# Three seams of a fused decoder layer: later weight quantisation, spread output products, and the feed-forward's first tile quantised one phase earlier

## The reference

```
x = x + self_attention(layernorm(x))            # 16 heads, window 128, sink, grouped output weights
x = x + cross_attention(layernorm(x), context)  # 16 query heads on 4 key heads, 1024 keys, slopes, then @ Wo
x = x + feed_forward(layernorm(x))              # silu(x @ gate) * (x @ up), Hadamard transform, @ down

# feed_forward: every input row is quantised to 8 bits, every weight matrix to three values
act_quant(x):    scale = 128 / max(|x|);         clip(round(x * scale), -128, 127) / scale
weight_quant(w): scale = 1 / mean(|w|);          clip(round(w * scale), -1, 1) / scale
```

## Time and profile before

| | us |
|---|---|
| median of 3 runs | 1656.32 (1654.77 to 1656.93) |
| the profiled execution's own time | 1656.29 |
| span of the profiled execution, first to last instruction | 1654.4 |
| self-attention, markers of steps 0 and 63 | 82.1 and 596.5 |
| cross-attention, first product and last residual row | 612.2 and 1335.4 |
| feed-forward, start | 1336.9 |
| PE busy over the span | 1566.2 (95%) |

### The profile page before, as it was taken

The page is one execution under the profiler, slowest core; times in us unless marked ns, Lnnn a source line. Parts: engine busy times, 40 slices in busy tenths (PEclk is TensorE's granted clock), DMA queues, the critical chain, the costliest instruction groups (busy, mean ns, idle before and its releaser), DMA issues. The chain is left out here.

```text
span 1654.4 us, 23944 instructions
## 1 busy us (share of the span) xinstructions
PE 1566.2 (95%) x7520; PEld 1072.2 (65%) x7520; DVE 1222.6 (74%) x2240; ACT 1186.7 (72%) x1962; POOL 1271.4 (77%) x1138
## 2 busy tenths in 40 slices
PE   8899999999999987999999999999999878999996
PEld 4577777787787755666666666666656425666664
DVE  2489978878776756777877788788778556767765
ACT  2354567777544435999999889989999726877875
POOL 0387767787777723899999999999999928888880
PEclk9999999999999998999999999999999989999999
DMA  7224254332300004210311032102203130110000
GB/s 257 92 80 88 90 136 121 111 122 90 102 20 8 32 18 119 92 46 20 112 39 58 25 107 58 33 19 59 58 13 117 43 114 1 34 33 26 33 14 26
DMA packets 57190, 110.24 MB, mean 67 GB/s; under 512 B 9244, under 2 KB 13596, under 8 KB 56682
## 3 DMA queue, kind: packets, MB, share of 16 engines
q1 hardware_dynamic: 55488, 107.64, 21.2%
q10 hardware_dynamic: 1578, 1.07, 0.2%
HBM read 71.26 MB, written 18.88 MB: 54 GB/s over the span
## 5 line engine op out<-in xcount | busy, mean ns | idle before, releaser
L1374 POOL TENSOR_TENSOR x_p_lo<-x_p,x_p_hi 128x1024 fp32r<-128x1024 f32 x256 | 606.4, 2393 | 62.7 <-ACT x_p_hi L1176 38.4
L1308 DVE TENSOR_REDUCE x_maxes<-x_ps_a 128x1 f32<-128x1024 f32 x252 | 306.6, 1217 | 121.7 <-PE x_ps_a L1459 117.9
L1149 ACT ACTIVATE x_p<-x_ps_b,x_any_valid 128x1024 f32<-128x1024 f32 x256 | 285.1, 1114 | 57.3 <-PE x_ps_b L1439 52.5
L1176 ACT ACTIVATE x_p_hi<-x_p 128x1024 fp32r<-128x1024 f32 x256 | 271.4, 1060 | 6.4
L1439 PE MATMUL x_ps_b<-x_Q,x_K 103*128 103x512 f32 x512 | 216.6, 504 | 9.0 <-ACT x_p L1149 7.2
L1493 PE MATMUL x_ps_o<-x_p_hi,x_V 128*96 128x512 f32 x512 | 209.7, 410 | 4.2 <-POOL x_p_lo L1374 4.2
L1494 PE MATMUL x_ps_o<-x_p_lo,x_V 128*96 128x512 f32 x512 | 202.8, 396 | 0.0
L1459 PE MATMUL x_ps_a<-x_K,x_Q 99*128 99x512 f32 x504 | 168.0, 414 | 11.3 <-DVE x_maxes L1308 8.4
L440 ACT ACTIVATE a_aT_hi<-a_ps_a 128x512 fp32r<-128x512 f32 x64 | 38.3, 598 | 169.5 <-PE a_ps_a L723 146.3
L1439 PEld LDWEIGHTS x_ps_b<-x_Q,x_K 103*128 103x128 f32 x512 | 87.4, 190 | 99.6 <-issue 55.3
L1459 PEld LDWEIGHTS x_ps_a<-x_K,x_Q 99*128 99x128 f32 x504 | 88.8, 190 | 54.4 <-DVE x_maxes L1308 31.9
(11 more groups left out here) (263 smaller groups left out, 4007.3 us busy)
## 6 DMA issues: line engine op xcount, KB each, us to landing
shared<-in_L_ffn_w_gate SPq DMA_DIRECT2D x16, 512.0 KB, 4.3
shared<-in_L_ffn_w_up SPq DMA_DIRECT2D x16, 512.0 KB, 4.1
shared<-in_L_ffn_w_down SPq DMA_DIRECT2D x16, 512.0 KB, 4.4
shared<-in_ctx SPq DMA_DIRECT2D x8, 1024.0 KB, 8.0
x_scratch<-rows SPq DMA_DIRECT2D x31, 256.0 KB, 2.0
x_Q<-x_q_hi SPq DMA_DIRECT2D x112, 64.0 KB, 2.0
shared<-in_L_attn_out_w SPq DMA_DIRECT2D x6, 1024.0 KB, 8.2
ffn_quant<-shared SPq DMA_DIRECT2D x24, 256.0 KB, 4.5
```

The lines of the kernel that those rows point to most:

```text
L1149: act.activation(p[:, v % 3, :, :], ps_b[:, :, :], ACT.Exp, scale=any_valid[:, b % 2:b % 2 + 1]).then_inc(exp_ready, 1)
L1176: act.activation(p_hi[:, r], p[:, v % 3], ACT.Copy).then_inc(hi_ready, 1)
L1308: dve.tensor_reduce(out=maxes[:, c % 2, 3 + r:4 + r], in_=scores_bank(n)[:, :, :], axis=mybir.AxisListType.XY, op=ALU.max).then_inc(max_re ...
L1374: pool.tensor_tensor(out=p_lo[:, v % 3], in0=p[:, v % 3], in1=p_hi[:, r].bitcast(F32), op=ALU.subtract).then_inc(lo_ready, 1)
```

## The change

1. **Weight quantisation.** Load, round, clip, clip and store of chunk k move eight steps later (steps k + 22, k + 24, k + 25, k + 26), and the ring `f_quant` has four places in place of two. The first loads of cross-attention move from step 44 to step 52.
2. **End of cross-attention.** The last batch's output products of groups k = 0, 1 and 2 are spread over units (62, 0) to (64, 1). The inversions of group 14 come in units (61, 3) and (62, 0) to (62, 2), and its `normalise` in (62, 3). The last group is normalised and multiplied in four blocks of 128 columns.
3. **First tile of the feed-forward.** Its layer norm, row maximum, rounding and clipping are made in units (62, 3) to (64, 1) of cross-attention, in `hq_first` and `first_max`. The feed-forward's steps start at -1, with the transposes of `hq_first`.

```diff
@@ self-attention
-        f_quant = shared[:, 6144:7168].bitcast(BF16).rearrange("p (s n) -> p s n", s=2)
+        f_quant = shared[:, 6144:8192].bitcast(BF16).rearrange("p (s n) -> p s n", s=4)
@@ SP
-                if 0 <= c - 18 < FFN_CHUNKS:
-                    store_quant(c - 18)
-                if 0 <= c - 14 < FFN_CHUNKS:
-                    load_raw(c - 14)
+                if 0 <= c - 26 < FFN_CHUNKS:
+                    store_quant(c - 26)
+                if 0 <= c - 22 < FFN_CHUNKS:
+                    load_raw(c - 22)
-                if c == 44:
-                    for j in range(2):
-                        sp.wait_ge(f_stored[j], 16 * (FFN_CHUNKS // 2))
+                if c == 52:
+                    for j in range(4):
+                        sp.wait_ge(f_stored[j], 16 * (FFN_CHUNKS // 4))
@@ ACT (the round and the clip, the same shift for both)
-                if 0 <= c - 16 < FFN_CHUNKS:
-                    k = c - 16
+                if 0 <= c - 24 < FFN_CHUNKS:
+                    k = c - 24
-                    if k >= 2:
-                        act.wait_ge(f_stored[k % 2], 16 * (k // 2))
+                    if k >= 4:
+                        act.wait_ge(f_stored[k % 4], 16 * (k // 4))
@@ DVE
-                if 0 <= c - 17 < FFN_CHUNKS:
+                if 0 <= c - 25 < FFN_CHUNKS:
@@ cross-attention, the spread products
+        last_out = {(HEADS - 2, 0): ((0, 0),), (HEADS - 2, 1): ((0, 2),), (HEADS - 2, 2): ((0, 3),), (HEADS - 2, 3): ((1, 0),),
+                    (HEADS - 1, 0): ((0, 1),), (HEADS - 1, 1): ((1, 2),), (HEADS - 1, 2): ((1, 3),), (HEADS - 1, 3): ((1, 1),),
+                    (HEADS, 0): ((2, 0), (2, 1)), (HEADS, 1): ((2, 2), (2, 3))}
@@ ACT, in the order of a unit: exponential, ACT's copy of PV, then this, then p_hi
+                if (c, r) == (HEADS - 1, 2):
+                    act.wait_ge(first_bias_ready, 1)
+                    act.wait_ge(job_made, jobs_until("Q", 3, B - 1))
+                    act.activation(first_row, ffn_x[0], ACT.Identity, scale=ln_rstd[:, 0:1], bias=ln_bias[:, 0:1]).then_inc(first_row_ready, 1)
+                if (c, r) == (HEADS, 0):
+                    act.wait_ge(first_max_ready, 3)
+                    act.activation(first_row, first_row, ACT.Copy, scale=first_max[:, 2:3], bias=MAGIC).then_inc(first_round_ready, 1)
+                if (c, r) == (HEADS, 1):
+                    act.wait_ge(first_round_ready, 1)
+                    act.activation(hq_first[:, :], first_row, ACT.Relu, scale=-1.0, bias=clip_bias[:, :])
@@ DVE
-                if r == 3 and c >= 5:
+                if r == 3 and 5 <= c < HEADS - 2:
                     inverse((c - 5) // HPG, (c - 5) % HPG)
+                if c == HEADS - 2 and r < 3:
+                    inverse(HEADS // HPG - 2, r + 1)
+                if (c, r) == (HEADS - 2, 3):
+                    dve.wait_ge(ffn_x_in[0], 16)
...
+                    dve.bn_stats(out=stats[:, 0, :], in_=ffn_x[0]).then_inc(stats_ready, 1)
+                    dve.wait_ge(stats_ready, TPB * B + 1)
+                    dve.bn_aggr(out=mv[:, 0, :], in_=stats[:, 0, :]).then_inc(first_mv_ready, 1)
+                if (c, r) == (HEADS - 1, 1):
+                    dve.wait_ge(first_rstd_ready, 1)
+                    dve.tensor_scalar(ln_bias[:, 0:1], mv[:, 0, 0:1], ln_rstd[:, 0:1], -1.0, ALU.mult, ALU.mult).then_inc(first_bias_ready, 1)
+                if (c, r) == (HEADS - 1, 3):
+                    dve.wait_ge(first_row_ready, 1)
+                    dve.tensor_reduce(out=first_max[:, 0:1], in_=first_row, axis=AXX, op=ALU.max, apply_absolute_value=True)\
+                        .then_inc(first_max_ready, 1)
...
+                    dve.tensor_scalar(first_max[:, 1:2], first_max[:, 0:1], EPS_Q, 1.0 / QB, ALU.max, ALU.mult).then_inc(first_max_ready, 1)
...
+                    dve.reciprocal(first_max[:, 2:3], first_max[:, 1:2]).then_inc(first_max_ready, 1)
@@ POOL, after the unit's p_lo
-                if r == 3 and c >= 8 and c % HPG == 0:
+                if r == 3 and 8 <= c < HEADS and c % HPG == 0:
                     normalise((c - 8) // HPG)
+                if (c, r) == (HEADS - 2, 3):
+                    normalise(HEADS // HPG - 2)
+                if (c, r) == (HEADS - 1, 0):
+                    pool.wait_ge(first_mv_ready, 1)
+                    pool.tensor_tensor(out=ln_var[:, 0:1], in0=mv[:, 0, 1:2], in1=eps[:, 0:1], op=ALU.add).then_inc(first_var_ready, 1)
+                    pool.wait_ge(first_var_ready, 1)
+                    pool.tensor_tensor(out=ln_rstd[:, 0:1], in0=ln_var[:, 0:1], in1=half_neg[:, 0:1], op=ALU.pow).then_inc(first_rstd_ready, 1)
-            normalise(HEADS // HPG - 1)
+            for k in range(TPB):
+                cols = slice(k * P, (k + 1) * P)
+                pool.wait_ge(inv_ready, 4 * G + k + 1)
+                pool.tensor_tensor(out=aT[:, G % (GX + 1), cols], in0=num[:, G % 2, cols], in1=den[:, G % 2, cols], op=ALU.mult).then_inc(aT_ready, 1)
@@ PE, in a unit after its PV
+                for k, i in last_out.get((c, r), ()):
+                    G = GX * (B - 1) + k
+                    pe.wait_ge(aT_ready, G + 1)
...
+                    pe.matmul(last_banks[i], aT[:, G % (GX + 1), i * P:(i + 1) * P], wo_sb[:, k, :], start=(k == 0), stop=False)
@@ PE, after the loop (in place of all 16 products)
+            for i in range(TPB):
+                pe.wait_ge(aT_ready, G + i + 1)
+                pe.matmul(last_banks[i], aT[:, G % (GX + 1), i * P:(i + 1) * P], wo_sb[:, GX - 1, :], start=False, stop=True).then_inc(job_made, 1)
@@ feed-forward
-        steps = range(-5, NQ + 18)
+        steps = range(-1, NQ + 18)
-                    pe.wait_ge(hq_ready, m + 1)
+                    if m:
+                        pe.wait_ge(hq_ready, m)
-                        last = pe.transpose(ps_q[:, a, :], hq[:, a * P:(a + 1) * P], ident_bf[:, :])
+                        last = pe.transpose(ps_q[:, a, :], (hq if m else hq_first)[:, a * P:(a + 1) * P], ident_bf[:, :])
```

More of the change, by code:

```diff
@@ L247, in phase_self_attention @@
         f_raw_in = [sem(f"f_raw_in{j}") for j in range(2)]
-        f_stored = [sem(f"f_stored{j}") for j in range(2)]
+        f_stored = [sem(f"f_stored{j}") for j in range(4)]
         f_sum_out, f_all_in = sem("f_sum_out"), sem("f_all_in")
@@ L454, in _ @@
                     act.activation(sink_exp[:, c % 2, :], sink_arg[:, c % 2, :], ACT.Exp).then_inc(sink_exp_ready, 1)
-                if 0 <= c - 16 < FFN_CHUNKS:
-                    k = c - 16
+                if 0 <= c - 24 < FFN_CHUNKS:
+                    k = c - 24
                     act.wait_ge(f_round_ready, k + 1)
-                    if k >= 2:
-                        act.wait_ge(f_stored[k % 2], 16 * (k // 2))
-                    act.activation(f_quant[:, k % 2, :], f_raw[:, k % 2, :], ACT.Relu, scale=-1.0, bias=f_clip[:, :])\
+                    if k >= 4:
+                        act.wait_ge(f_stored[k % 4], 16 * (k // 4))
+                    act.activation(f_quant[:, k % 4, :], f_raw[:, k % 2, :], ACT.Relu, scale=-1.0, bias=f_clip[:, :])\
                         .then_inc(f_clip_ready, 1)
@@ L858, in phase_cross_attention @@
         x1t = rows
+        clip_bias = sb("clip_bias", [P, 1])
+        first_row = hT[:, 1, :]
         ps_a = ps("ps_a", (P, 2, 512))
@@ L889, in phase_cross_attention @@
             sem(n) for n in ("o_copied", "den_copied", "num_ready", "inv_ready", "aT_ready"))
+        first_mv_ready, first_var_ready, first_rstd_ready, first_bias_ready, first_row_ready, first_max_ready, first_round_ready = (
+            sem(n) for n in ("first_mv_ready", "first_var_ready", "first_rstd_ready", "first_bias_ready", "first_row_ready",
+                             "first_max_ready", "first_round_ready"))
         UNITS = [(c, r) for c in range(-2, HEADS + 1) for r in range(4)]
@@ L1506, in _ @@
                         before += 1
+                for k, i in last_out.get((c, r), ()):
+                    G = GX * (B - 1) + k
+                    pe.wait_ge(aT_ready, G + 1)
+                    if k == 0:
+                        if i == 0:
+                            pe.wait_ge(job_read, before)
+                        if i == 1:
+                            pe.wait_ge(max_row_ready, HEADS)
+                        if i >= 2:
+                            pe.wait_ge(max_ready, 4 * HEADS)
+                    pe.matmul(last_banks[i], aT[:, G % (GX + 1), i * P:(i + 1) * P], wo_sb[:, k, :], start=(k == 0), stop=False)
                 if norm_of(c, r):
@@ L1516, in _ @@
                     norms += 1
-            banks = (ps_j[:, :], ps_x[:, :], ps_a[:, 0, :], ps_a[:, 1, :])
-            pe.wait_ge(job_read, before)
-            pe.wait_ge(max_row_ready, HEADS)
-            pe.wait_ge(max_ready, 4 * HEADS)
-            for k in range(GX):
-                G = GX * (B - 1) + k
-                pe.wait_ge(aT_ready, G + 1)
-                for i in range(TPB):
```

(11 more changed lines are left out.)

66 lines of the change are left out of this document (39 added, 27 removed).

## The result

The changed kernel takes 1639.38 us, the median of four runs (1637.48 to 1640.03), against 1655.55 for four runs of the kernel before, taken beside it (1653.37 to 1656.93). The ratio is 0.9902, with a 95% interval from 0.9884 to 0.9919: 16.2 us faster. The forecast was 1637.5, from 18.8 us of gain. The profiled execution took 1639.33, and its span is 1637.5.

What follows compares the result with a forecast made beforehand. It took as bounds ACT's store waits in self-attention, POOL and then PE's leftover products ending cross-attention, and the first tile's chain starting the feed-forward. 1656.3 - 10.5 - 5.5 - 2.8 = 1637.5 us, range 1632 to 1645.

Steps and rivals of the forecast that it cites:

- The quantisation: Self-attention, first batch: ACT's clips no longer wait for `f_quant` stores; gain 10.5 us, at most 11.
- the slack of two steps: Self-attention: store of chunk k - 4 issued two steps, 16 us, before it is needed, so ACT's wait goes.
- the separated loads: Self-attention: absolute-sum loads end in step 21, second loads begin in step 22, so they no longer share DMA engines.
- DVE not short of time: Self-attention, first batch: DVE busy for 59 of 73 us, so not what holds the batch up.
- The end of cross-attention: Cross-attention's tail: last residual row at 1330.6 in place of 1336.08, gain 5.5 us.
- PE's last product takes 1.0 with its drain: End of cross-attention: after the last block's multiply PE finishes at 1329.4; DVE's residual rows set the end, 1330.6.
- rival A: Cross-attention's tail: PE's clock falls, giving 1640.5 us, or 1646.8 if to the block's end; 17 in 100.
- The feed-forward's start: First tile made early: products soon after T (start of the feed-forward's loads), ACT waits for the Hadamard matrix; gain 2.8 us.
- Gain 2.8: Feed-forward's start: silu(1) at T + 9.4 against T + 12.2 before; bounds 1.5 and 5.6 us.
- The sum: Whole kernel: 1656.3 less gains of 10.5, 5.5 and 2.8 gives 1637.5 us.
- the third term: Feed-forward's start: the gain of 2.8 us from making the first tile in cross-attention.
- Rival B: Feed-forward's start gains all 5.6 us, by earlier matrix landing or full clock: 1634.7, at best 1632; 14 in 100.

Runs made afterwards that it cites:

- e1: Kernel before plus only the quantisation change (eight steps later and ring of four): 1643.99 us, ratio 0.9934.
- e2: Kernel before plus only the ring of four for `f_quant`, no step moved: 1647.20 us, ratio 0.9951.
- e3: Kernel before plus only the shift of quantisation by eight steps, ring of two kept: 1643.53 us, ratio 0.9935.
- e7: Changed kernel plus twelve unused score products on PE between its last PV and the last four output products: 1639.50 us, ratio 0.9908.
- e5: Changed kernel with the Hadamard matrix loaded in cross-attention, not at the feed-forward's start: 1630.90 us, and 1629.30 once more.
- e4: Changed kernel without the early first tile, which is quantised in the feed-forward as before: 1638.14 us, ratio 0.9904.
- e11: Changed kernel without the early first tile, but with the Hadamard matrix loaded in cross-attention: 1639.47 us, ratio 0.9904.

## Why the prediction was right, and where it wasn't

**The quantisation** was right in mechanism and size: 10.5 foreseen, 10.4 in the markers, 10.9 by e1's ratio; no wait for a store, 129.46 us against "about 129". The sum was not touched by what e2 and e3 add: the prediction gave the slack of two steps as the reason and the separated loads as a bonus, while either half alone would have won most of it. It also called DVE not short of time, from a busy share of 59 in 73 us; with the ring alone PE stands for DVE 2.80 us (e2), so the shift wins something on DVE's side too.

**The end of cross-attention** was right up to the inversions. Counted from the end of unit 251's `p_lo` (1299.53), the last `p_lo` ends at 11.6 (foreseen 11.8), the last PV at 13.2 (13.35), the inversions at 18.1 (18.2), and ACT's idle time is 3.23 (3.4). The step that was mis-sized is the last: "PE's last product takes 1.0 with its drain". The first two pairs took 2.00 and 1.89 each at the lower clock, so the last row came at 22.4 in place of 20.9, and 3.9 were won where 5.5 were foreseen (4.1 when counted from the exponential of unit 254 to T). That is a small form of rival A. The prediction looked for the clock's fall where only PV is left; it came behind the hole of 3.10 us that the spreading itself makes, while POOL and DVE work on the last group. e7 filled that hole, and the same products ran at 1.00. The rule that it quoted against A was "activity releases the throttle" (the Trainium skill, "TensorE: Matmul & The Clock Gate", Part 1). The traces of after and e7 agree with it, read from its other side: a rest was followed by 0.50, work by 1.00. But in e5 the same hole of 3.11 us was followed by 1.00, so the rule alone does not say what one hole will cost.

**The feed-forward's start** was right in its steps: landing 8.5 us after issue (8.7 foreseen), products at T + 1.2 (1.3), ACT idle for 5.41 (about 5), silu(1) at T + 9.05 (9.4). The Trainium skill ("DMA: Bandwidth & Descriptors", "Issuing engines are not separate DMA queues") says that DMAs which the scalar, sync and GpSimd engines issue run on the same 16 DMA engines and interleave. The trace agrees: the matrix on ACT's queue landed (8.5 us) with SP's 2 MB (8.3 us) and not ahead of it. The step that failed is "Gain 2.8", and for two reasons. First its base: 12.2 us to silu(1) was read from one profile, in which the first twelve products all ran at the lower clock (until 1348.8); e1 repeats that, but in e2, e3, e4 and e11, with the same products, the lower clock ends after eight of them or fewer, and it is 10.9 to 11.4. That leaves a head start of some 2.0. Second, it doesn't last. Counted from T, DVE's product f, numbered from 0, comes as number 1 at 9.8 in after and at 12.3 in e4; number 3 at 15.7 and 17.7; number 6 at 25.3 and 27.3; number 7 at 30.8 and 31.4; number 13 at 55.5 and 56.1. Of the 2.5 us 0.5 are lost behind PE's wait (clock 0.50 from 1333.0) and 1.4 between numbers 6 and 7, where after's clock is low again from 1350.1 and e4's isn't; 0.6 are left. From T to the end the six profiles with the old start average 316.1 (314.9 to 317.5), the five with the new start and the late matrix 315.7 (314.7 to 316.5). Part 3 wins 0.4 there, less than the spread of either group, and costs 0.7 to 1.1 in the tail. The forecast's 2.8 and the 2.8 of the profiled pair agree by chance.

**The sum** still lay within 1.9 us, as the parts that hold it are 10.9 and 5.0; of the 18.8 us foreseen 16.2 were measured, and what is missing is the third term. **Rival B** named the remedy for part 3, a matrix that lands sooner, and e5 shows that it was under-priced too: 8.3 and 9.9 us below after's 1639.2 against the 2.8 that B gave. At the same mean clock it is 4.6: silu(1) comes 4.75 us earlier, not 2.8. The rest is the clock: without the wait PE has no hole there, and the profile no lower clock.

Open is what makes DVE late in e2, and what decides in which of these places the clock falls in one execution: e5's profile has one stretch at 0.50 in the cross-attention's start and none in the tail or the feed-forward's start, after's has two, one and two there, and six runs of after spread from 1635.4 to 1642.2.

## What to carry to other kernels

Before work is pulled out of a phase's start, look for the next thing that was hidden beneath it: here a 256 KB load that nobody waited for turned 5.6 us of removed work into 0.4, and moving that load as well made it 7, part of it by the clock. A gain that one pair of profiles shows in one phase counts only once other kernels with the same code in that phase show it; here the base itself moved by 2.6 us (314.9 to 317.5). Two remedies for one wait (a deeper ring, a later start) are not two gains. And before a median is put down to an edit, compare runs with the same mean granted clock: here that made 4.6 us of 8.3.

## What the hardware showed that was not expected

- A hole of 3 to 5 us in PE's work was followed by a stretch at 1.2 GHz in after (1315.9 behind 3.10 us, 1333.0 behind 4.73), and it cost 1.5 us in the first place and 0.5 in the second; in e5 the same hole of 3.11 us was followed by products at 2.4 GHz.
- Filling one hole with twelve unused products (2.90 us) kept the next products at 2.4 GHz and brought the lower clock into the next phase's: no net gain.
- 256 KB issued beside 2 MB landed after 8.5 us; the stores of the same size to the output and of x2 took 2.0 us in the median.
- The tiny operations of POOL were 0.18 us (add) and 0.56 us (power) on 128x1, and a quarter of the 1.28 us multiply took 0.46 us.
